# First layer: the last convolution tap of two of three groups, one scan tile later on VectorE

## The reference, cut to what matters

```
z, xBC, dt = split(x @ in_proj_w.T)            # widths 256, 288, 4
xBC = silu(causal_conv(xBC, conv_w, 4 taps) + conv_b)
xs, B, C = split(xBC)                           # 256, 16, 16
h[t] = h[t-1] * dA[t] + dt[t] * B[t] (x) xs[t]  # per head, 4 heads of 64
y[t] = C[t] . h[t] + Dp * xs[t]
out  = rmsnorm(y * silu(z)) @ out_proj_w.T
```

## Time and profile before

| | |
|---|---|
| median of 3 runs | 2875.7 us (2871.59 to 2876.74) |
| span of the profiled execution | 2867.6 us, 8.1 us under the median |
| instructions | 44223 |
| busy: PE, DVE, ACT, POOL | 78%, 58%, 43%, 25% of the span |
| first layer, 0 to 600 us | DVE 405.37 us busy, PE 453.57 us busy |

### The profile page before, as it was taken

How to read it: one execution, slowest core, us unless ns; L and a number is a source line. 1 busy time by engine, 2 the same in 40 slices (tenths; PEclk the granted TensorE clock), 3 DMA queues, 4 the chain that set the end, 5 groups by cost and what they waited for, 6 DMA issues and landing times. The chain is left out here.

```text
span 2867.6 us, 44223 instructions
## 1 busy us (share of the span) xinstructions
PE 2232.3 (78%) x15437; PEld 1302.5 (45%) x15454; DVE 1650.8 (58%) x3303; ACT 1246.7 (43%) x1901; POOL 727.9 (25%) x870
## 2 busy tenths in 40 slices
PE   3778878863899989999740389999999788777474
PEld 2555555542344444444340134444443686455274
DVE  6676767631677747567049277777775343553201
ACT  2343434320466656565520046565666343332143
POOL 1435353441010101000000223233322113663432
PEclk8898888876899999999755599999999899896597
DMA  2111100012011101110000302121210895110185
GB/s 62 39 53 53 46 2 2 2 44 85 2 55 40 54 24 32 46 36 20 1 1 3 106 22 77 42 79 40 79 54 27 257 321 185 41 41 22 38 274 182
DMA packets 144303, 185.77 MB, mean 65 GB/s; under 512 B 26970, under 2 KB 118267, under 8 KB 138976
## 3 DMA queue, kind: packets, MB, share of 16 engines
q1 hardware_dynamic: 103295, 137.52, 16.0%
q0 software_dynamic: 13696, 32.02, 3.5%
q10 hardware_dynamic: 27126, 13.75, 1.7%
HBM read 130.46 MB, written 52.21 MB: 64 GB/s over the span
## 5 line engine op out<-in xcount | busy, mean ns | idle before, releaser
L1743 DVE TENSOR_REDUCE a_mpart<-a_mx 128x1 f32<-128x512 f32 (+3 forms) x1216 | 741.2, 655 | 284.4 <-PE a_mx L1497 148.8
L1653 ACT ACTIVATE a_prob<-a_st 128x1024 f32<-128x1024 f32 (+3 forms) x768 | 607.1, 812 | 487.8 <-PE a_st L1533 374.4
L1497 PE MATMUL a_mx<-a_ka,a_qa 96*128 96x512 bf16 (+3 forms) x1536 | 428.8, 339 | 31.6 <-DVE a_mpart L1743 14.4
L1530 PE MATMUL a_st<-a_qa,a_ka 96*128 96x512 bf16 (+3 forms) x1536 | 416.3, 333 | 29.9 <-ACT a_prob L1653 22.8
L1548 PE MATMUL a_acc<-a_prob,a_v_aug 128*9 128x512 f32 (+3 forms) x3072 | 321.1, 494 | 0.0
L1497 PEld LDWEIGHTS a_mx<-a_ka,a_qa 96*128 96x128 bf16 x1536 | 140.7, 99 | 315.6 <-DVE a_mpart L1743 175.4
L1426 POOL DMA_INDIRECT x_rows<-l_xn,l_slots x128 | 125.4, 980 | 400.0 <-ACT a_prob L1653 390.0
L1533 PE MATMUL a_st<-w_mask_t,identb 128*128 128x128 bf16 x1024 | 208.8, 224 | 0.0
L1530 PEld LDWEIGHTS a_st<-a_qa,a_ka 96*128 96x128 bf16 x1536 | 145.7, 99 | 136.5 <-ACT a_prob L1653 38.6
L2084 PE MATMUL t_psu<-t_xsT,t_w 128*128 128x128 f32 x960 | 152.8, 294 | 23.9 <-DMA t_w<-in_l_experts 17.4
L1500 PE MATMUL a_mx<-w_mask_q,identb 128*128 128x128 bf16 x768 | 165.2, 225 | 0.0
(11 more groups left out here) (438 smaller groups left out, 4055.0 us busy)
## 6 DMA issues: line engine op xcount, KB each, us to landing
t_w<-in_l_experts SPq DMA_DIRECT2D x160, 192.0 KB, 4.2
t_w<-in_l_experts SPq DMA_DIRECT2D x40, 514.0 KB, 7.4
a_qa<-q_parts_dram SPq DMA_DIRECT2D x96, 192.0 KB
a_ka<-k_parts_dram SPq DMA_DIRECT2D x96, 192.0 KB
x_rows<-zeros SPq DMA_DIRECT2D x25, 512.0 KB, 3.6
t_xs<-x_rows ACTq DMA_DIRECT2D x40, 256.0 KB, 4.9
y_rows<-t_y POOLq DMA_DIRECT2D x40, 256.0 KB, 5.1
q_parts_dram<-a_parts SPq DMA_DIRECT2D x24, 256.0 KB, 3.0
```

The source lines that it names most:

```text
L1497: ins = pe.matmul(to, qa[G % NQ][:, h0 + k, qi * P:(qi + 1) * P], ka[G % NQ][:, h0 + k, lo:hi], start=not masked_first, stop=k == per - 1 ...
L1530: ins = pe.matmul(to[:, lo:HALF], ka[G % NQ][:, h, j * P:(j + 1) * P], qa[G % NQ][:, h, ch * HALF + lo:(ch + 1) * HALF], start=True, stop= ...
L1653: act.activation(prob[:, v % NP_, 2 * pair:2 * pair + 2, lo:HALF], sring[s % 2][:, :, lo:HALF], ACT.Exp, scale=1.0 if alibi else scale).th ...
L1743: dve.tensor_reduce(mpart[:, G % 2, h0:h0 + per, qi, piece], slot[:, 0:per * width].rearrange("p (k w) -> p k w", k=per), X, ALU.max).then ...
```

## The change

For groups 0 and 1 of units 1 to 7 the last tap (back = 3) becomes an event of its own, `last_tap`. VectorE runs it at position 1.03 past the tile of its convolution, which lies between `m` (1.02) and `gate` (1.04) of the next tile. The release of the ring slot goes with it. The silu of these groups moves from +0.75 to +1.15 in ScalarE's order. Unit 0 and group 2 stay. No arithmetic is added or taken away.

```diff
--- before.py
+++ after.py
@@ -275,10 +275,13 @@
                            (7.6, "ts_cut"), (7.8, "da_turn")):
                 put(pos + at_, (e, b))
 
+        def parted(u, k):
+            return u > 0 and k < 2
+
         def unit_jobs(u, pos):
             for k in range(3):
                 put(pos + k - 0.1, ("conv", u, k))
-                put(pos + k + 0.75, ("silu", u, k))
+                put(pos + k + (1.15 if parted(u, k) else 0.75), ("silu", u, k))
             put(pos + 2.15, ("first", u))
             put(pos + 2.6, ("start", u))
             for half, pair, at_ in ((0, 0, 3.2), (0, 1, 3.65), (1, 0, 4.65), (1, 1, 5.65)):
@@ -350,7 +353,9 @@
                 return pos + 0.3
             return min(pos + 0.3, math.floor(pos) + 0.99) if e[0] in by_dve else pos
 
-        dve_order = [e for _, e in sorted(timed, key=lambda v: behind(*v))]
+        dve_timed = [(behind(*v), v[1]) for v in timed]
+        dve_timed += [(math.floor(pos) + 1.03, ("last_tap", *e[1:])) for pos, e in dve_timed if e[0] == "conv" and parted(*e[1:])]
+        dve_order = [e for _, e in sorted(dve_timed, key=lambda v: v[0])]
         ring_at = {e: i for i, e in enumerate(ring_order)}
         fin_order = [e for e in order if e[0] == "fin"]
         fin_at = {e: i for i, e in enumerate(fin_order)}
@@ -868,17 +873,22 @@
                             link(dve.tensor_tensor_scan(tile_at[:, 2], tile_at[:, 0], tile_at[:, 1], float(BATCH * T - P), ALU.mult, ALU.add))
                             dve.tensor_scalar(row_id[:], tile_at[:, 2], partition[:], None, ALU.add).then_inc(ids_set, 1)
                             dve.wait_ge(ids_set, 1)
-                        elif kind == "conv":
+                        elif kind in ("conv", "last_tap"):
                             _, u, k = e
-                            dve.wait_ge(tapped, 3 * u + k + 1)
+                            if kind == "conv":
+                                dve.wait_ge(tapped, 3 * u + k + 1)
                             to = conv[:, k] if k < 2 else cT[:, u % 2]
-                            for back in range(1, TAPS):
-                                ins = dve.scalar_tensor_tensor(to[:, back:], flat(e)[:, 0:T - back],
+                            backs = list(range(1, TAPS))
+                            if parted(u, k):
+                                backs = backs[:-1] if kind == "conv" else backs[-1:]
+                            for back in backs:
+                                ins = dve.scalar_tensor_tensor(to[:, back:], flat(("conv", u, k))[:, 0:T - back],
                                                                W["cw_xc"][:, u % 2, k, TAPS - 1 - back:TAPS - back], to[:, back:],
                                                                ALU.mult, ALU.add)
                                 if back + 1 < TAPS:
                                     link(ins)
-                            ins.then_inc(ring_v, 1)
+                            if TAPS - 1 in backs:
+                                ins.then_inc(ring_v, 1)
                         elif kind == "first":
                             u = e[1]
                             if u:
```

## The result

The kernel with the change took 2883.01 us (median of 14 runs, 2873.07 to 2893.93), the kernel before on the same chip 2875.09 us (14 runs, 2869.88 to 2884.79). The ratio is 1.0031, its 95% interval 1.0017 to 1.0045: slower by 8.9 us (4.9 to 12.9). The prediction was 2884.8 us, 9.1 us slower. A second set of 12 runs of the same kernel gave 1.0019 (1.0005 to 1.0034); one run of the kernel before in that set, 3660.47 us at a granted clock of 0.56, was in a slow state and is left out of every figure here. The two profiled executions have spans of 2867.6 us (before) and 2881.5 us (after); that they are 13.9 us apart and not 8.9 is looked at further down.

What follows compares the result with a forecast made beforehand. The prediction took TensorE's group 1 projection, held by z and the shared ring slot, to set the gate. Group 0's 10.1 us less unit 1's 1.0 gave 9.1 us over 2875.7, so 2884.8 us, likeliest 2882 to 2887.

Steps and rivals of the forecast that it cites:

- What bounds the kernel: Units 2 to 7: TensorE's group 1 projection, held level by z and the shared slot, sets the gate; VectorE idles 2.04 us.
- Group 0 of units 2 to 7, +10.1 us: The later last tap delays group 1's projection and the gate by 1.68 us a unit; bounds 9.1 to 10.1 us.
- The first term, 1.51 us: Group 0, units 2 to 7: the last tap ends at 163.88 against 162.37 before, 1.51 us later.
- The second term, 0.17 us: Group 1's projection starts 0.26 us behind the tap's end from a stop, against 0.09 before; bounds 0 and 0.17.
- Group 1 of units 2 to 7, 0 us: No neighbour needs the slot soon; first is delayed about 4 us, covered by group 2's taps; cost 0 us.
- Unit 1, -1.0 us: Groups 0 and 1 have different slots; group 2 starts 1.12 us earlier, or 0.90 with a longer m; taken as 1.0.
- ScalarE, 0 us: Units 2 to 7: the silu stands ahead of the norm's root; 0.7 us of cover left, cost 0.
- Does it reach the end?: The delay carries through the first layer, ending it 8 to 10 us later; later layers last as long as before.
- Sum: 10.1 - 1.0 = 9.1 us; span 2867.6 becomes 2876.7, median 2875.7 becomes 2884.8, with 8.1 us around the span untouched.
- Busy share: Rival: VectorE's work is unchanged, late gates meet slack, only unit 1's gain stays, 2874.7; absorbed wholly or by half: 0.15.
- The gap is filled: Rival: the last tap lies in VectorE's 2.04 us idle before the gate, faster by 8.4 us, 2867.3; chance 0.05.
- The clock falls: Rival: stops of about 1.5 us ahead of six projections lower TensorE's clock; 2891.7 if in two units; chance 0.12.

Runs made afterwards that it cites:

- the new ring order and the moved taps: Kernel after with second z projection behind next unit's group 2, first and start behind the scores in units 2 to 7; 2885.86 us, ratio 1.0029.
- the new ring order: Kernel before with second z projection behind next unit's group 2, first and start later in units 2 to 7, silus at +1.15; 2862.9 us, ratio 0.9952.
- unit 1 alone: Against the kernel before, only unit 1's last taps moved, groups 0 and 1; 2870.65 us, ratio 0.9997.
- group 0 alone: Against the kernel before, only group 0 of units 2 to 7 has its last tap moved; 2885.48 us, ratio 1.0046.
- group 1 alone: Against the kernel before, only group 1 of units 2 to 7 has its last tap moved; 2870.31 us, ratio 0.9996.
- the added instruction: Kernel after plus one unused VectorE product of 1.22 us ahead of group 0's last tap from unit 2 on; 2902.32 us, ratio 1.0059.

## Why the prediction was right, point by point

- **What bounds the kernel.** Right: TensorE's projection of group 1, held level by `z` and by the slot, sets the gate. With the shared slot and `z` taken away, the idle goes to 0.24 us with whole taps and 0.20 with moved ones.
- **Group 0 of units 2 to 7, +10.1 us.** Right in mechanism. The first term, 1.51 us for the later end of the tap, measured 1.57: from the first tap's start to the last one's end are 5.47 us (159.80 to 165.27) and were 3.90; the stretch from the copy of sums to the tap took 1.56 us (162.43 to 163.99), 0.05 more than worked out. The second term, 0.17 us for a start from a stop, was mis-sized and is 0: the projection starts 0.05 us behind the tap's end and not 0.26, and the gate is 3.50 us behind that start where it was 3.46. The row that it was taken from, the small matmuls behind the end of `m`, was not a near one; why their start takes longer wasn't tried. Measured 1.56 to 1.58 us a unit and 9.4 us in all, within the bounds of 9.1 to 10.1.
- **Group 1 of units 2 to 7, 0 us.** Right. TensorE stands 2.82 us ahead of `first` (175.83 above) and the next three gates (10, 11, 12) show steps of 0.00, 0.13 and 0.08 us against the kernel before; alone the part gave 0.9996. One number in it was worked out wrong: the delay of `first` was put at about 4 us, but by the prediction's own rows the last tap moves from an end at 170.17 to one near 172.8, some 2.7 us. It measured 2.70 (175.83 against 170.23, at a gate 9 that is 2.90 later). The cover of some 4 us was right: VectorE asked for it at 179.84. The cover is that no job which VectorE or the scan wants soon stands in that slot; with the new ring order and the moved taps it was gone, and the kernel that should have been at -13.8 us was at +8.3.
- **Unit 1, -1.0 us.** This term was mis-sized: it is 0. The working inside the unit was right (1.15 us against 1.12), but the prediction had no term for what comes behind. Four groups of matmuls at the lower clock took back all of it within one tile, in all seven profiled executions with these taps moved. With unit 1 alone the last gate is level with before to 0.07 us counted from gate 0, and the median, -0.9 us with an interval of 9 us, doesn't contradict it.
- **ScalarE, 0 us.** Right. In the kernel after, the first tap started at 167.35, the root ended at 171.11, and group 1's two taps on VectorE at 171.75 (169.16 + 2.59): 0.64 us of cover, worked out as 0.7.
- **Does it reach the end?** Yes: no later tile won the steps back. At gate 63 the kernel after is 10.6 us and its second profile 9.5 us late, where the prediction had 8 to 10 as its sign.
- **Sum.** +9.1 forecast, +8.9 measured; made from the terms as the traces show them it is 9.4. Two errors of opposite sign, 0.7 us too much for the steps and 1.0 us too much for the gain of unit 1, nearly cancel, and the agreement to 0.2 us is luck at an interval of 8 us. The 13.9 us between the two spans is 10.6 us in the first layer and 3.3 us in layers whose code is the same. What lies around the span is 1.7 us in the execution of the kernel after (2883.18 against 2881.5), and 2.0 us in runs of the kernel before that have both figures (2880.56 against 2878.6). So most of the 8.1 us that the prediction had put there was the profiled execution of before being a fast one. It didn't matter to a sum of differences.
- **The rivals.** *Busy share* would have given 2874.7; group 0 alone against group 1 alone decides against it. The rule that the prediction named from the Trainium skill (Perfetto Trace Analysis, section Identifying the Most-Contended Engine) would look at the busy share of VectorE, or at that of TensorE's weight loads. The trace disagrees with what follows from it here: the two shares stayed at 57 to 58% and 45%, and the time did change. *The gap is filled* was seen nowhere: with the shared slot the tap delays the gate, and with another one the gap is gone before it. *The clock falls* at the six projections was not seen in either profile of the kernel after, but it was in two of six with 1.13 us more of stop; in unit 1 it took the forecast gain back.

## What to carry to other kernels

Before a reader's last instruction is moved, look up who takes over the buffer it releases: with r - NA as the rule of the ring that is one line of arithmetic, and the engine that waits there has everything else in its order queued behind. Idle time in front of an instruction is only free for work that this idle doesn't itself depend on; a release belongs ahead of the gap, and work without a release may lie in it. If a move hurts through a shared slot, try the order of the ring instead of the order of the engine: here that gained 0.5% where the moved tap lost 0.3%.

## What the runs showed of the hardware

- TensorE picks up from a stop as fast as from a running queue: 0.05 us from the end of VectorE's tap to the load and the first matmul (165.27 to 165.32, and 164.92 to 164.97 with the added instruction), where the kernel before, with `z` in the array, had 0.09.
- Stops of like length leave the clock high in one place and low in another: 1.37 us left it high in six units of six, 2.50 us lowered it in two of six. With the new ring order and the moved taps 3.00 us left it high in three of three, and behind 3.68 us the projection was slow in three of three, by 0.6 to 1.8 us against the 1.99. One and the same stop of 2.63 us, ahead of group 0's projection of unit 2, was followed by a projection of 1.94 us in the kernel before and of 2.89 us in the kernel after. What decides was not found.
- Single executions are spread. Between the profiled ones the time from gate 63 to the end, where all kernels have the same code, runs from 2244.3 to 2263.9 us, twice the whole effect that was to be measured. The first layer is steadier: two executions of the kernel after agree in every gate to 0.24 us once they are laid on gate 0, and differ by 7.3 us behind gate 63. A difference of 9 us in this kernel is read from the steps at named instructions and from medians of a dozen runs, not from two spans.
- The last instruction of `m` takes 0.48 us as a rule and up to 1.29 us in places. In the kernel before it took 0.66 to 1.26 us in 12 of its 56 occurrences, and in all 12 GpSimd was at work on a TENSOR_TENSOR at the same time; in a few others that overlapped too it took 0.48 to 0.54. What the two share wasn't tried.
